# Layer 1's rows of maxima issued by another engine, and the projection of v spread over later steps

## The chip, the cores and the metric

The kernel runs on one core of one Trainium2 chip. The metric is the time of one execution on the device, in microseconds (us). Below, PE is TensorE (PEld its weight loads), DVE is VectorE, ACT is ScalarE, POOL is GpSimd and SP is SyncE. SPq and ACTq are the DMA issues of those two engines.

## What is computed

Two transformer-like layers on x of shape (8, 512, 256), in float32. This study is about layer 1's attention, which is causal and runs twice over the same keys and values:

```
qkv = xn @ Wqkv.T + b                     # 16 heads of 16 dimensions
q, k, v = split(qkv)
ctx  = causal_softmax(q @ k.T / 4) @ v
q2   = conv1d(ctx, width 3) + conv_b
ctx2 = causal_softmax(q2 @ k.T / 4) @ v
x    = x + ctx2 @ out_w.T + out_b + low_rank_ffn(xn)
```

Layer 0, which comes first, has plain attention and an eight-expert feed-forward part; the change does not touch its instructions.

## The kernel before

**Units and rounds.** Layer 1's attention is cut into 32 units: kind 1 (first attention) or kind 2 (second), batch element `b`, and half `c` (8 of the 16 heads). The order alternates two kind-1 units and two kind-2 units. `layer1` runs one round per unit and interleaves, step by step, four lanes: the exponentials of unit i (`expp`), the row maxima of unit i+1 (`maxp`), the preparation of unit i+2 (`pre1`) and the output of unit i-1 (`fin1`). A round has 22 steps. Every engine walks through the same program and issues its own part of each step, so the order of instructions on each engine's queue is the order of the steps. Within a step the lanes come in the order given.

**Preparation.** Queries and keys are float32 values split into three bf16 parts. ACT writes the high part (`high`), DVE the remainder (`residue`, L1345), POOL the two lower parts (`low`, L2014 and L2016). Then SP copies the parts into the operand tiles QA and KA by six DMAs for q and six for k (`fan`, tile t_spl to t_R; `start` at L2143 issues all DMAs of SP). A kind-1 unit also stores its split keys to memory (`ks`, one DMA behind the twelve). A kind-2 unit gets q from the convolution (L1216) and k back from `ks`. The projection of v is four parts of PE (L1197) in steps 10 to 13, and one addition of DVE (L1362) in step 14.

**Row maxima.** A unit has two halves g of 4 heads. `top` makes scores with PE (L978) and reduces them on DVE (L1387), 11 steps for each half. Then `shift` runs as a chain of its own beside the following tops: two steps later PE transposes the maxima (`turn_m`, L997) and DVE splits their negatives into three bf16 rows (`split_m`, L1401 to L1409, tile t_msp). One step after that `rows` copies the three rows into partitions 96 to 98 of QA by three DMAs of 4 KB. For half 0 this is step 14 of the round before the unit's exponentials, for half 1 step 3 of their own round. SP issues them in layer 0 and in layer 1:

```
e.wait_ge(s.msp_done, 2 * u.n + g + 1)
for x in range(3):
    self.start(m.QA[u.buf][96 + x:97 + x, 4 * g:4 * g + 4, :], m.msp[:, x, :], s.d_mq[u.buf][g])
```

**Exponentials.** PE makes the transposed scores with the rows included (`scores`, L1011, and the mask at L1015), into two banks used in turn: the scores of step k+2 wait for ACT's exponential of step k (L1812). PE's first scores of a half (steps 0 and 11) wait for that half's rows (d_mq). The sixteen products with v of a half go in one go two steps after its last scores (`product`, L1028, tile p_PV): step 12 for half 0, and step 1 of the next round for half 1. PE's `top` of step 0 waits for the copies of q and k (d_f) of the unit that follows.

Of the kernel before, what the change touches and what calls it, by code (L numbers as in the profile page):

```python
# [81 lines left out]
def packs_of(u):  # L82

    if u.causal:
        return [(0, (0, 1, 2, 3)), (1, (0, 1)), (1, (2, 3))] + [(qb, (j,)) for j in range(4) for qb in (2, 3)]
    return [(qb, (j,)) for j in range(4) for qb in range(4)]
# [76 lines left out]
def steps(n):  # L163
    for _ in range(n):
        yield
# [345 lines left out]
class Engine:  # L511
# [115 lines left out]
    def routing(self):  # L627
        return steps(46)
# [51 lines left out]
    def maxp0(self, u):  # L680
        return steps(s1_uses(u))
# [25 lines left out]
    def rows(self, u, g): pass  # L707
# [19 lines left out]
    def pre1(self, u):  # L727

        if u.kind == 1:
            yield from steps(3)  # L730
            self.part(u, 0, 0)
            yield
            self.part(u, 0, 1)
            yield
            self.high1(u, 0)
            yield
            self.rest(u, 0)
            self.part(u, 1, 0)
            yield
            self.part(u, 1, 1)  # L740
            yield
            self.fan1(u, 0)
            self.high1(u, 1)
            yield
            self.rest(u, 1)
            yield
            for k in range(4):
                self.part(u, 2, k)
                if k == 1:
                    self.fan1(u, 1)  # L750
                yield
            self.values(u)
            return
        soon = u.c or u.b not in (0, NB - 1)
        yield from steps(3 if u.c else 1 if soon else 6)
        if u.c == 0:
            for c in range(2):
                self.turn_c(u, c)
                yield
                self.keep_c(u, c)  # L760
                yield
        for i in range(6):
            self.convolve(u, i)
            if i == 3:
                self.fan1(u, 1)
            if soon or i % 2:
                yield
        self.high1(u, 0)
        yield
        self.rest(u, 0)  # L770
        yield
        self.fan1(u, 0)
        yield
# [948 lines left out]
class ScalarE(Engine):  # L1722
# [94 lines left out]
    def copy_o(self, u, g):  # L1817
# [3 lines left out]
        e.wait_ge(s.oT_mm, i - 32)  # L1821
        nc.scalar.copy(m.O[:, :], m.PV[:, :]).then_inc(s.pv_read, 1)

    def routing(self):
        e, m, s = self.e, self.m, self.s
        yield
        e.wait_ge(s.amax, 1)
        self.nc.scalar.activation(m.alpha[:, :], m.amax, ACT.Exp, scale=-1.0).then_inc(s.alpha_exp, 1)
        yield from steps(45)
# [290 lines left out]
class SyncE(Engine):  # L2120
# [59 lines left out]
    def maxp0(self, u):  # L2180
        for g in range(2):
            yield from steps(len(packs_of(u)))
            self.rows(u, g)
            yield

    def rows(self, u, g):
        e, m, s = self.e, self.m, self.s
        e.wait_ge(s.msp_done, 2 * u.n + g + 1)
        if 3 <= u.n < 16 or u.n >= 19:
            e.wait_ge(s.pv_mm, 8 * (u.n - 2))  # L2190
        for x in range(3):
            self.start(m.QA[u.buf][96 + x:97 + x, 4 * g:4 * g + 4, :], m.msp[:, x, :], s.d_mq[u.buf][g])
# [149 lines left out]
```

## Time and profile before

| | |
|---|---|
| median of 3 runs | 2215.4 us (2213.17 to 2216.7) |
| profiled execution | 2214.24 us, its span 2212.4 us |
| PE busy, share of span | 83% |
| DVE / ACT / POOL busy | 56% / 46% / 16% |
| mean granted clock of TensorE | 0.907 of full speed |
| layer 1's attention in the trace | about 1230 to 2212 us |

The span runs from the first to the last instruction; 1.8 us of the profiled execution lie around it. Shares of busy time are averages over the whole program.

### The profile page before, as it was taken

The page shows a single profiled execution, that of the slowest core. Times are in us where ns is not written, and L with a number is a line of the kernel's source. Part 1 is how long each engine was busy: PE and PEld are TensorE (multiplying, and loading weights), DVE is VectorE, ACT ScalarE, POOL GpSimd, SP SyncE. Part 2 cuts the span into 40 slices and gives each one's busy share as a digit, 9 for nine tenths or more (in the row PEclk, how much of TensorE's full clock was granted, in tenths as well). Part 3 has the DMA queues.
Part 4 walks back from the last instruction along what each step waited for, and adds up shares of the span by engine and source line. Part 5 has one row for each costly group of instructions (what it writes and reads, how often), then busy time and mean ns, then how long its engine had stood idle before and what let it go on. Part 6 is the DMA issues. An engine that isn't in the chain of part 4 may idle for free.

```text
span 2212.4 us, 31852 instructions
## 1 busy us (share of the span) xinstructions
PE 1844.8 (83%) x10767; PEld 938.3 (42%) x10777; DVE 1243.9 (56%) x3777; ACT 1016.5 (46%) x2048; POOL 364.4 (16%) x555
## 2 busy tenths in 40 slices
PE   3584899999979999993788878888878898888877
PEld 2341444554525454541233434444444444444434
DVE  4554555565554454544544656665766656565653
ACT  0232456565635555562343434444444444444434
POOL 2215211111111111114432100000100101000000
PEclk8566899999989999996898889998989998998999
DMA  7244343334374444413104424443444533543430
GB/s 144 65 151 126 73 80 69 81 73 79 61 203 64 63 64 67 63 23 93 34 19 63 61 43 66 69 64 59 63 66 67 73 55 52 74 66 52 69 44 21
DMA packets 145968, 155.87 MB, mean 70 GB/s; under 512 B 26008, under 2 KB 132784, under 8 KB 145808
## 3 DMA queue, kind: packets, MB, share of 16 engines
q1 hardware_dynamic: 123872, 114.75, 31.9%
q0 software_dynamic: 10048, 14.44, 3.6%
q10 hardware_dynamic: 11888, 24.64, 3.5%
q8 instruction: 88, 1.44, 0.3%
q14 instruction: 72, 0.59, 0.1%
HBM read 55.95 MB, written 33.72 MB: 41 GB/s over the span
## 4 chain that ended last, share of the span: by engine, by line
PE 53%; DVE 11%; SPq 11%; DMA 10%; issue 6%; POOL 6%; ACT 2%; DVEq 0%; POOLq 0%; ACTq 0%
PE p_PV L1028 11%; SPq L2143 11%; PE p_S L1011 7%; DMA t_R<-t_msp 6%; PE p_S L961 4%; PE p_Ma L1216 4%; PE p_Mb L1078 4%; PE p_S L1101 3%; DVE p_S L1387 3%; PE p_S L978 2%; POOL t_spl L2016 2%; POOL idd L2042 1%; PE p_Mb L1101 1%; DMA t_xTb<-xTd 1%; PE p_Ma L938 1%
## 5 line engine op out<-in xcount | busy, mean ns | idle before, releaser
L1812 ACT ACTIVATE t_R<-p_S 128x512 f32<-128x512 f32 (+1 forms) x1216 | 680.6, 578 | 706.3 <-PE p_S L1015 541.2
L1387 DVE CUSTOM_DVE_ANT_0 p_S<-p_S,t_NM 128x128 f32<-128x128 f32 (+3 forms) x1024 | 478.4, 514 | 347.8 <-PE p_S L978 344.3
L1011 PE MATMUL p_S<-t_R 99*128 99x512 bf16 (+3 forms) x1536 | 479.7, 337 | 100.5 <-DMA t_R<-t_msp 82.4
L1373 DVE TENSOR_REDUCE t_mx<-p_S 128x1 f32<-128x512 f32 x512 | 346.1, 685 | 257.5 <-PE p_S L961 241.1
L1028 PE MATMUL p_PV<-t_R 128*17 128x512 f32 (+3 forms) x3072 | 334.7, 561 | 1.0 <-ACT t_R L1812 1.0
L978 PE MATMUL p_S<-t_R 96*128 96x128 bf16 (+3 forms) x1024 | 264.4, 313 | 43.3 <-DVE t_mx L1387 26.0
L1011 PEld LDWEIGHTS p_S<-t_R 99*128 99x128 bf16 x1536 | 150.7, 99 | 239.1 <-DMA t_R<-t_msp 91.7
L961 PE MATMUL p_S<-t_R 96*128 96x512 bf16 x512 | 206.1, 405 | 19.9 <-DVE t_mx L1373 18.9
L2014 POOL CAST t_spl<-t_rr 128x512 bf16<-128x512 f32 x80 | 49.8, 622 | 1022.4 <-DVE t_rr L1345 1022.4
L1015 PE MATMUL p_S<-t_NM 128*128 128x128 bf16 x1024 | 203.2, 224 | 0.0
L1028 PEld LDWEIGHTS p_PV<-t_R 128*17 128x17 f32 x3072 | 77.8, 107 | 198.2 <-issue 186.7
L978 PEld LDWEIGHTS p_S<-t_R 96*128 96x128 bf16 x1024 | 88.7, 102 | 132.1 <-DVE t_mx L1387 67.6
L1387 DVE DVE_READ_ACCUMULATOR2_ANT t_mx<- 128x1 f32 x1024 | 142.4, 139 | 0.0
L961 PEld LDWEIGHTS p_S<-t_R 96*128 96x128 bf16 x512 | 50.8, 100 | 194.0 <-issue 97.5
L1015 PEld LDWEIGHTS p_S<-t_NM 128*128 128x128 bf16 x1024 | 102.5, 100 | 67.9 <-issue 44.9
L1078 PE MATMUL p_Mb<-t_R,t_NM 128*128 x184 | 97.0, 608 | 7.5 <-DMA t_NM<-hTd 3.2
L1101 PE MATMUL p_S<-t_R,t_NM 128*128 x392 | 100.9, 379 | 0.0
L1216 PE MATMUL p_Ma<-t_NM,t_R 128*128 128x512 f32 x192 | 98.1, 596 | 0.7 <-ACT t_NM L1922 0.6
L2016 POOL TENSOR_TENSOR t_spl<-t_rr,t_spl 128x512 bf16<-128x512 f32 x80 | 92.7, 1159 | 6.4
L1101 PEld LDWEIGHTS p_S<-t_R,t_NM 128*128 128x128 f32 x392 | 73.8, 190 | 17.9 <-issue 2.3
L1896 ACT ACTIVATE t_R<-p_S,t_R 128x512 f32<-128x512 f32 x64 | 43.5, 687 | 61.7 <-PE p_S L1147 51.6
L2066 POOL DMA_DIRECT2D ysd<-t_NM x39 | 34.1, 875 | 208.7 <-ACT t_NM L1868 208.7
(244 smaller groups left out, 2180.9 us busy)
## 6 DMA issues: line engine op xcount, KB each, us to landing
t_R<-t_spl SPq DMA_DIRECT2D x480, 128.0 KB
t_R<-in_w ACTq DMA_DIRECT2D x32, 512.0 KB, 7.3
t_R<-ks SPq DMA_DIRECT2D x96, 128.0 KB
ks<-t_spl SPq DMA_DIRECT2D x16, 384.0 KB, 6.9
hTd<-t_NM SPq DMA_DIRECT2D x39, 128.0 KB
ysd<-t_NM SPq DMA_DIRECT2D x39, 128.0 KB
t_NM<-hTd SPq DMA_DIRECT2D x39, 128.0 KB, 2.2
ysd<-t_NM POOLq DMA_DIRECT2D x39, 128.0 KB, 3.1
```

The costliest lines, as they stand in the source:

```text
L961: self.nc.tensor.matmul(m.S1[s1_bank(k)][:, :], qa[0:96, 4 * g + j, qb * 128:(qb + 1) * 128], ka[0:96, 4 * g + j, 0:512], start=True, stop ...
L978: t = self.nc.tensor.matmul(bank[:, z, :], qa[0:96, h, qb * 128:(qb + 1) * 128], ka[0:96, h, 0:n], start=True, stop=True)
L1011: t = self.nc.tensor.matmul(bank[:, z, :], ka[0:99, h, kb * 128:(kb + 1) * 128], qa[0:99, h, n0:512], start=True, stop=not u.causal)
L1015: t = self.nc.tensor.matmul(bank[:, z, 0:128], m.identb, m.maskk, start=False, stop=True)
L1028: t = self.nc.tensor.matmul(m.PV[32 * j:32 * j + 17, n0:512], vt[:, kb, 4 * g + j, :], m.p_tile(u, g, kb, j), start=(kb == 0), stop=(kb == 3),
L1078: z = self.nc.tensor.matmul(m.MB[i][:, :], m.hT[t % 2][:, c, :], m.W1[:, bass.ds(self.regs[t], 1), c, :], start=(c == 0), stop=(c == 1))
L1101: x = self.nc.tensor.matmul(M[:, 0:256], m.AT[:, k, :], m.W2[:, bass.ds(self.regs[t], 1), k * 256:k * 256 + 256], start=(k == 0), stop=(p ...
L1216: t = self.nc.tensor.matmul(m.MB[0][:, :], m.CW[:, i, c * 128:c * 128 + 128], m.cT[:, cc, k:k + 512], start=(i == 0), stop=(i == 5))
L1373: nc.vector.tensor_reduce(m.mx[:, g, 4 * j + qb:4 * j + qb + 1], m.S1[s1_bank(k)][:, :], AX.X, ALU.max).then_inc(s.s1_read, 1)
L1387: x = nc.vector.tensor_tensor_reduce(out=sc, in0=sc, in1=m.maskq[:, 512 - n:512], scale=1.0, scalar=NEG, op0=ALU.add, op1=ALU.max, accum_o ...
L1812: nc.scalar.activation(m.P1X[kb][ring_use(u, g, j0) % 6 if kb == 0 else j0 // per] if u.causal else m.P[p % 2][:, j0:j0 + per, :], m.s2_ba ...
L2143: self.raw.dma_start(to, of).then_inc(sem, 16)
```

## The change

`rows` in layer 1 moves from SP's queue to ACT's, with the same waits and the same three DMAs; layer 0's copy of it stays on SP under the name `rows0`. In `pre1` for kind-1 units, the four parts of the projection of v move from steps 10, 11, 12 and 13 to steps 12, 14, 16 and 18, and DVE's addition of `values` from step 14 to step 20. The copy of the keys, `fan1(u, 1)`, stays at step 11. `rest(u, 1)` stays at step 9.

```
@@ Engine.pre1, kind 1
             self.rest(u, 1)
             yield
+            yield
+            self.fan1(u, 1)
+            yield
             for k in range(4):
                 self.part(u, 2, k)
-                if k == 1:
-                    self.fan1(u, 1)
+                yield
                 yield
             self.values(u)
@@ ScalarE, new
+    def rows(self, u, g):
+        e, m, s = self.e, self.m, self.s
+        e.wait_ge(s.msp_done, 2 * u.n + g + 1)
+        if u.n >= 19:
+            e.wait_ge(s.pv_mm, 8 * (u.n - 2))
+        for x in range(3):
+            self.raw.dma_start(m.QA[u.buf][96 + x:97 + x, 4 * g:4 * g + 4, :], m.msp[:, x, :]).then_inc(
+                s.d_mq[u.buf][g], 16)
@@ SyncE
-            self.rows(u, g)
+            self.rows0(u, g)
...
-    def rows(self, u, g):
+    def rows0(self, u, g):
...
-        if 3 <= u.n < 16 or u.n >= 19:
+        if u.n >= 3:
```

## Rows read from the trace of the kernel before

**Rows 1.** The page's chain that ended last, by engine and by line.
```profile
PE 53%; DVE 11%; SPq 11%; DMA 10%; issue 6%; POOL 6%; ACT 2%; DVEq 0%; POOLq 0%; ACTq 0%
```

**Rows 2.** Waits in 1230:2212: us in total, times, longest us.
```profile
ACT t_R L1812 <- PE p_S L1015: 522.0, 397, 7.3
PE p_S L1011 <- DMA t_R<-t_msp: 82.4, 28, 5.2
```

**Rows 3.** PE's timeline at four round ends: start, duration, instruction, [idle before <-releaser].
```profile
1526.95 0.61 PE L1011 MATMUL p_S<-t_R 99*128 99x512 bf16 x1 [3.79 <-DMA t_R<-t_msp]
...
1528.56 4.26 PE L1028 MATMUL p_PV<-t_R 128*17 128x512 f32 x32
...
1587.94 0.39 PE L1011 MATMUL p_S<-t_R 99*128 99x512 bf16 x1 [1.62 <-DMA t_R<-t_msp]
...
1588.82 2.35 PE L1028 MATMUL p_PV<-t_R 128*17 128x512 f32 x32
...
1611.70 0.38 PE L978 MATMUL p_S<-t_R 96*128 96x512 bf16 x1
1616.49 0.61 PE L1011 MATMUL p_S<-t_R 99*128 99x512 bf16 x1 [4.41 <-DMA t_R<-t_msp]
```

**Rows 4.** Windows of 100, 3 and 1 us: busy, then PEclk, DMA share, GB/s.
```profile
1600.00:1700.00 100.00, 84.89 (x632) 46.42 (x634) 62.61 (x249) 44.28 (x84) 8.19 (x10) 0.91 0.49 70
...
1467.00:1470.00 3.00, 3.00 (x20) 0.99 (x24) 1.10 (x8) 1.19 (x2) 0.00 (x0) 0.60 0.00 0
...
1531.00:1532.00 1.00, 1.00 (x16) 0.28 (x12) 0.00 (x0) 0.00 (x0) 0.00 (x0) 0.50 0.00 0
```

**Rows 5.** SP's queue: start, time of the group, tile, number of DMAs.
```profile
1599.65 7.75 SPq L2143 DMA_DIRECT2D t_R<-t_spl  x12
1607.44 0.60 SPq L2143 DMA_DIRECT2D ks<-t_spl  x1
1608.09 1.81 SPq L2143 DMA_DIRECT2D t_R<-t_msp  x3
```

**Rows 6.** Windows of half a microsecond at the end of that round.
```profile
1613.50:1614.00 0.50, 0.00 (x0) 0.00 (x0) 0.00 (x0) 0.00 (x0) 0.00 (x0) 1.00 0.79 307
...
1614.50:1615.00 0.50, 0.00 (x0) 0.00 (x0) 0.00 (x0) 0.00 (x0) 0.00 (x0) 0.50 0.12 36
```

**Rows 7.** DMA to landing of three rows each, issued from 1568.1, 608.1 and 633.8.
```profile
DMA to landing us min/median/max: 1.6/1.7/1.7
...
DMA to landing us min/median/max: 4.0/4.2/4.5
...
DMA to landing us min/median/max: 7.8/7.9/8.0
```

**Rows 8.** Issues of rows on SP and of weights on ACT: ns min/median/max.
```profile
L2143 SPq DMA_DIRECT2D t_R<-t_msp x186: 502/589/1807, 1240.1 to 2181.9; - x186
...
L1774 ACTq DMA_DIRECT2D t_R<-in_w x16: 374/374/408, 148.4 to 646.2; - x16
```

**Rows 9.** Timelines of DVE and PE, steps 2 and 6 of a kind-1 round.
```profile
1593.89 0.28 DVE L1409 TENSOR_TENSOR t_msp<-t_mrr,t_msp 16x128 bf16<-16x128 f32 x1
...
1595.63 0.33 PE L1011 MATMUL p_S<-t_R 99*128 99x384 bf16 x1
```

**Rows 10.** ACT and PE, steps 4 and 5 of a kind-2 round with c = 0.
```profile
1536.43 0.49 ACT L1812 ACTIVATE t_R<-p_S 128x384 f32<-128x384 f32 x1 [0.47 <-PE p_S L1015]
1536.82 0.58 ACT L1922 COPY t_NM<-p_Ma 128x512 f32<-128x512 f32 x1
...
1537.45 1.12 PE L1216 MATMUL p_Ma<-t_NM,t_R 128*128 128x512 f32 x2
```

**Rows 11.** Steps 13 to 17, kind-1 round: DVE's last split, PE's scores of step 17.
```profile
1607.16 0.28 DVE L1409 TENSOR_TENSOR t_msp<-t_mrr,t_msp 16x128 bf16<-16x128 f32 x1
...
1607.63 0.33 PE L1011 MATMUL p_S<-t_R 99*128 99x384 bf16 x1
```

**Rows 12.** PE's groups in 1230:2212: busy us, mean ns, idle before.
```profile
L1197 PE MATMUL p_Ma<-t_WQ,t_R 128*128 128x128 f32 x224 | 34.8, 278 | 0.0
```

## Prediction

> **What bounds the kernel now.** I read the chain that ended last first. PE holds 53% of it, but SP's queue and DMA together hold 21% [rows 1]: the end is set in part by transfers and their issue. So I went to the waits in the stretch of layer 1's attention. ACT is idle for 522 us of it, always for PE's scores: that is slack, not a bound. What costs is PE's wait for the rows of maxima: 82.4 us in 28 waits, about one in each round [rows 2]. PE's timeline shows where: at step 0 of a round, before the first scores. Fourteen of the waits are long (4.41 and 3.79 us are two of them) and end the rounds that prepare a kind-1 unit; the other fourteen are short (1.62 us is one) and end the kind-2 rounds [rows 3]. By their mean the long ones make about 14 x 4.0 = 56 us and the short ones 26 us.
>
> The wait has a second price. After a long one the sixteen products take 4.26 us where they take 2.35 us after a short one [rows 3], and in that second the granted clock is 0.50, the 1.2 GHz level, where PE had been on the 2.4 GHz level before it idled [rows 4]. A stretch of 100 us with a mean clock of 0.91 has 18 us at half speed [rows 4], some 5 to 6 us a round; PE work done in it costs double. From the wait's end at 1526.95 to the end of the products at about 1532.8 [rows 3] that is 2.9 us lost.
>
> Why the rows are late: in the round that ends at 1616.49, DVE had them ready at 1607.16 + 0.28 = 1607.44 [rows 11]. SP was still issuing twelve copies of q and k, then the store of the keys, and reached the rows at 1608.09, 0.65 us late [rows 5]. That is little. The landing is what takes long: three small DMAs issued by 1609.9 let PE go on at 1616.49 [rows 3, 5], while three such DMAs on a quiet queue land in 1.7 us [rows 7]. They stand in one queue behind 1.5 MB of copies and the store.
>
> **The change: the queue.** The rows leave SP's queue for ACT's. Issue: ready by 1607.44, three issues at 589 ns each on SP [rows 8], last one out near 1609.2. An issue on ACT is shown only for weights, 374 ns [rows 8]. The rows' form is nearer to SP's figure, so I take 1.8 us for three, with 1.1 us as the lower bound. Landing beside another queue's traffic is bounded by layer 0: rows on SP with only ACT's weight loads ahead landed in 4.2 us, rows with both queues full in 7.9 us [rows 7]. I take 4 us, since ACT's queue is empty here. So the rows land at 1612 to 1613, about when PE has finished step 21 (1611.70 + 0.38) [rows 3].
>
> The Trainium skill ("DMA: Bandwidth & Descriptors", "Queues, rings and completion order") says that each DMA engine takes turns between queues, packet by packet. By that rule the landing comes out early, which the 4.2 us bear out. The same page ("Issuing engines are not separate DMA queues") says that issuing from several engines saves only issue time; by that alone the gain would be the 0.65 us a round.
>
> **What is late next.** PE's tops of step 0 need the k copies of the next unit, and these stay where they were. The data rate jumps to 307 GB/s at 1613.5 [rows 6], when only the store is left, so the copies' data ended near 1613.2. From the end of the store's data, by 1614.6 at 36 GB/s [rows 6], to PE's start at 1616.49 [rows 3] are 1.8 us, so a completion takes about that, and k arrives near 1614.8. The long wait is thus shortened by 1.7 us, not by 4.0: 14 x 1.7 = 24 us. In kind-2 rounds six copies stand directly ahead of the rows, without a store. The rows are last by little, 0.5 us as I put it: 14 x 0.5 = 7 us. Together 31 us of the 82.
>
> **The clock.** A long wait of 4 us becomes about 2, near today's short ones. A short one can lose the clock as well: in the 3 us from a start at 1467.0 it was 0.60 [rows 4], so 2.4 us at half speed and 1.2 lost by then, while the products after the short wait at 1587.94 ran in full time [rows 3]. I take 1.5 us where it falls. So 14 x (2.9 - 1.5) = 20 us come back at the long ones. At the short ones the wait sinks to near 1 us; I let ten of them keep a clock that they lose today, 10 x 1.5 = 15 us (the ten is my guess). Sum 35 us, bounds 0 and 14 x 2.9 + 15 = 56 us.
>
> **What ACT pays.** Behind the three issues on ACT stand the exponentials, and PE's scores two steps later wait for those. Half 1, step 3, kind-1 round: rows ready at 1594.17 (1593.89 + 0.28), issues until 1596.0, so the exponential of step 4 (0.49 us for this form [rows 10]) runs 1596.0 to 1596.5. PE's scores of step 6 started at 1595.63 and now wait: 0.9 us [rows 9]. ACT's high part of q and the q copies slip as much, so nothing hides it: 14 x 0.9 = 13 us. Kind-2 round with c = 0: rows ready about 1536.0, issues to 1537.9, then the exponential and the copy of L1922 of 0.58 us, which the convolution at 1537.45 needs; it starts at 1539.0 [rows 10], 1.6 us late, 8 x 1.6 = 13 us. With c = 1 the convolution's matmuls fill PE meanwhile: nothing. Half 0, step 14, kind-1: the issues end at 1609.3 and PE's scores of step 17, at 1607.63 before [rows 11], come near 1609.9. That costs nothing at the round's end while PE would otherwise wait for k there; without that cover it costs up to 1 us a round, 30 us in all. Sum 26 us; with issues of 374 ns about 12, with all 62 stalls uncovered at 1.8 us each 112.
>
> **The projection of v.** The same sixteen matmuls: 34.8 us over 14 units, 0.62 us a part [rows 12]. Three parts fewer stand ahead of step 14, so the maxima of half 0 come up to 1.3 us sooner. Parts in steps 16 and 18 fall where PE waits for the delayed exponentials. DVE's addition moves by six steps; its next reader is units away and the bank is next wanted in step 1 or 3 of the following round. I count 0, bounds -1 us and +0.5 us a round (-14 and +7). `fan1(u, 1)` stays in step 11: 0. SP loses 186 issues and its waits on the maxima; the copies wait for POOL instead, so 0.
>
> **Sum.** The profiled execution took 2214.2 us, 1.2 below the median. 2214.2 - 31 - 35 + 26 = 2174, against the median 2175.
>
> **Rivals.**
> - *The clock stays up and ACT's stall is small.* The full 56 us of clock, 31 of waits, 12 of stalls, 14 for v: 2214 - 56 - 31 + 12 - 14 = 2125; with half of these extras 2150. For it: a 2 us wait is near the ones that cost little. Against: the weights' form is not the rows'.
> - *ACT becomes the bound (slower).* Place: steps 3 and 14, where the wait for DVE and 1.8 us of issues block the exponentials. The gains are 66 us over 62 halves, so it decides from a mean loss of 1.1 us a half. With 1.5 us: 2214 - 66 + 93 = 2241. For it: only two score banks. Against: ACT idles 522 us, and the convolution and k's wait cover half of the places.
> - *The rows land no sooner.* Landing of 7.9 us from 1608.2 [rows 7] is 1616: nothing gained, 26 paid: 2240. The skill's page (first section named) says that a completion is signalled only after the earlier writes of that DMA engine in any queue; if that reached to copies still queued, this is what it would do. The row of 4.2 us was measured with two loads in flight, so it doesn't exclude it.
> - *Gain and stall cancel:* 2211 to 2219.
>
> **Numbers.** Forecast 0.45 (own range 2150 to 2200), clock and small stall 0.23, ACT bound 0.12, late landing 0.11, cancel 0.09. A difference under 0.2% can't be told from none. Faster 0.68, same 0.09, slower 0.23. The range that leaves out at most 2 in 10 goes from 2120 to 2235.
>
> **What the profile should show.** Rows' waits at step 0 mostly gone; in kind-1 rounds a wait for t_spl of about 2 us in their place; L1812 held for ACT's queue in steps 3 and 14; PE scores of L1011 waiting for L1812 by some 25 us more; products after a round's start nearer to 2.35 than 4.26 us; landing of the rows about 4 us under the copies. Wrong if the rows land in 7 us, if PE's waits for L1812 pass 60 us, or if k is there before PE.

## The result, and the profile after

| | before | after |
|---|---|---|
| median in the comparison | 2214.28 us (2211.49 to 2216.95, 8 runs) | 2202.26 us (2197.87 to 2207.88, 8 runs) |
| ratio, 95% interval | | 0.9947 [0.9934, 0.996] |
| span of the profiled execution | 2212.4 us | 2199.9 us |
| layer 1 in the trace | 1218.96 to 2212.40: 993.4 us | 1213.71 to 2199.90: 986.2 us |

The kernel is 0.5% faster, 12 us, where 40 were forecast. The direction was right and the size was not.

Two lines were added to the file ahead of these places: L1011, L1015, L978, L1028, L1216 and L1812 of before are L1013, L1017, L980, L1030, L1218 and L1814 after. L1832 is the issue of the rows on ACT's queue.

The chain that ended last, by engine, against [rows 1]:

```profile
PE 58%; DVE 12%; DMA 10%; issue 6%; ACT 4%; POOL 4%; ACTq 4%; SPq 2%; DVEq 0%; POOLq 0%
```

SP's queue fell from 11% to 2%. ACT's queue rose from 0 to 4% and ACT from 2 to 4%: part of the path moved from one issuing engine to the other. DMA kept its 10%.

Waits in 1230:2213, as in [rows 2] (us in total, times, longest us):

```profile
PE p_S L1013 <- ACT t_R L1814: 77.9, 70, 3.8
PE p_S L1013 <- DMA t_R<-t_msp: 30.9, 14, 3.5
PE p_S L980 <- DMA t_R<-t_spl: 13.5, 7, 4.4
PE p_Ma L1218 <- ACT t_NM L1933: 9.1, 7, 1.5
PE p_S L980 <- DVE t_mx L1389: 1.0, 1, 1.0
```

Before, the same five stood at 4.7, 82.4, 13.3, 0.6 and 22.9 us. The wait for the rows shrank by 51.5 us. The wait for the exponentials grew by 73.2. PE's tops waited for DVE for 22.9 us in short waits; of these one is left, since PE now stands still elsewhere meanwhile.

PE in layer 1, from its first scores to the end. First before, then after (the sixth number is the clock, behind the busy times of PE, PEld, DVE, ACT and POOL):

```profile
1218.96:2212.40 993.44, 837.92 (x6191) 447.30 (x6191) 612.70 (x2438) 444.12 (x844) 77.98 (x88) 0.92 0.40 59
```

```profile
1213.71:2199.90 986.19, 825.59 (x6191) 460.05 (x6191) 622.80 (x2438) 439.62 (x844) 77.99 (x88) 0.93 0.42 60
```

The same 6191 matmuls take 12.3 us less, and PE is idle for 160.6 us instead of 155.5. So in this pair of traces layer 1 gained 7.2 us: all of it, and more, is PE's busy time, in which the mean granted clock rose from 0.92 to 0.93, and the waits together got worse by 5. The other 5.3 us of the spans' difference arise before layer 1's first scores, where the change touches only the preparation of the first units. That start lies between 1213.5 and 1223.2 in the kernels below without any order in it, so for causes I compare layer 1's part, and for verdicts the medians. Each such part is from one execution, and the eight of the changed kernel lie 10 us apart: differences of a few us between two traces are hints and no more.

PE's timeline over the end of one round that prepares a kind-1 unit, against [rows 3]:

```profile
1505.53 0.34 PE L1013 MATMUL p_S<-t_R 99*128 99x384 bf16 x1 [0.80 <-ACT t_R L1814]
...
1519.26 0.34 PE L1013 MATMUL p_S<-t_R 99*128 99x384 bf16 x1 [1.63 <-ACT t_R L1814]
...
1524.72 0.39 PE L1013 MATMUL p_S<-t_R 99*128 99x512 bf16 x1 [2.13 <-DMA t_R<-t_msp]
...
1525.60 2.35 PE L1030 MATMUL p_PV<-t_R 128*17 128x512 f32 x32
```

The round had one long wait; now it has three shorter ones: 0.80 behind half 1's rows (an exponential that ACT ran late), 1.63 behind half 0's, 2.13 for the rows. After the last the products ran in 2.35 us, so here the clock was kept, where [rows 3] shows 4.26.

ACT and its queue in the same place:

```profile
1516.86 1.80 ACTq L1832 DMA_DIRECT2D t_R<-t_msp  x3
1518.71 1.91 ACT L1814 ACTIVATE t_R<-p_S 128x384 f32<-128x384 f32 x4 [2.41 <-issue]
```

The three issues take 1.80 us, and the four exponentials that had piled up follow at once. SP in the same round, and the landing of those rows:

```profile
1509.48 8.83 SPq L2154 DMA_DIRECT2D t_R<-t_spl  x12
1518.36 0.60 SPq L2154 DMA_DIRECT2D ks<-t_spl  x1
```

```profile
t_R<-t_msp ACTq DMA_DIRECT2D x3, 4.0 KB, 6.6
```

The last number is the median from issue to landing. The rows' own queue was empty, they were issued from 1516.86, and they landed 6.6 us later. The round of [rows 5] now reads 7.7 to 8.1 us.

Did the rows arrive sooner, then? The first copy of q is the event to count from. SP in the same round before the change:

```profile
1510.80 9.53 SPq L2143 DMA_DIRECT2D t_R<-t_spl  x12
1521.02 1.81 SPq L2143 DMA_DIRECT2D t_R<-t_msp  x3
```

The rows were issued 10.2 us after the first copy before and 7.4 us after it now, 2.8 us sooner. PE went on 16.15 us after the first copy before (1526.95, [rows 3]) and 15.24 us after it now (1524.72), only 0.9 us sooner. In the round of [rows 5] it is 16.84 against 16.82 us, and over the 14 kind-1 rounds 16.4 against 15.7 us in the mean. (A kind-1 round here is one that prepares a kind-1 unit, and a kind-2 round one that prepares a kind-2 unit.) PE's waits in these rounds fell from 4.0 to 2.2 us in the mean. So 0.7 us of that is an earlier landing. The other 1.1 us is PE coming later to the same wait, held up by its new stalls.

### The profile page after: what moved, and what is told of

The parts are those of the page before. It is cut to its first block, busy times and chain, and to the rows that moved or that the text cites. A ratio compares the mean times of both kernels' runs of the same rounds, so it can differ in the third digit from the quotient of the medians.

```text
span 2199.9 us, 31862 instructions
## 1 busy us (share of the span) xinstructions
PE 1827.9 (83%) x10777; PEld 950.1 (43%) x10777; DVE 1253.7 (57%) x3777; ACT 1011.9 (46%) x2048; POOL 364.4 (17%) x555
## 4 chain that ended last, share of the span: by engine, by line
PE 58%; DVE 12%; DMA 10%; issue 6%; ACT 4%; POOL 4%; ACTq 4%; SPq 2%; DVEq 0%; POOLq 0%
PE p_PV L1030 12%; PE p_S L1013 8%; DMA t_R<-t_msp 4%; PE p_S L963 4%; PE p_S L980 4%; PE p_Ma L1218 4%; ACTq L1832 4%; PE p_Mb L1080 4%; PE p_S L1103 3%; DVE p_S L1389 3%; SPq L2154 2%; DMA t_R<-t_spl 2%; ACT t_R L1814 2%; PE p_S L1017 1%; POOL idd L2053 1%
## 5 line engine op out<-in xcount | busy, mean ns | idle before, releaser
L1814 ACT ACTIVATE t_R<-p_S 128x512 f32<-128x512 f32 (+1 forms) x1216 | 677.4, 578 | 686.2 <-PE p_S L1017 435.8
L1389 DVE CUSTOM_DVE_ANT_0 p_S<-p_S,t_NM 128x128 f32<-128x128 f32 (+3 forms) x1024 | 483.4, 511 | 325.7 <-PE p_S L980 321.2
L1013 PE MATMUL p_S<-t_R 99*128 99x512 bf16 (+3 forms) x1536 | 493.6, 346 | 122.6 <-ACT t_R L1814 83.6
L1030 PE MATMUL p_PV<-t_R 128*17 128x512 f32 (+3 forms) x3072 | 301.1, 512 | 1.0 <-ACT t_R L1814 1.0
L980 PE MATMUL p_S<-t_R 96*128 96x128 bf16 (+3 forms) x1024 | 274.2, 321 | 21.0 <-DMA t_R<-t_spl 13.5
L1013 PEld LDWEIGHTS p_S<-t_R 99*128 99x128 bf16 x1536 | 156.0, 103 | 280.8 <-ACT t_R L1814 143.7
L1017 PE MATMUL p_S<-t_NM 128*128 128x128 bf16 x1024 | 215.2, 234 | 0.0
L1030 PEld LDWEIGHTS p_PV<-t_R 128*17 128x17 f32 x3072 | 72.2, 100 | 169.7 <-issue 156.0
L1017 PEld LDWEIGHTS p_S<-t_NM 128*128 128x128 bf16 x1024 | 108.2, 106 | 68.2 <-issue 53.4
L980 PEld LDWEIGHTS p_S<-t_R 96*128 96x128 bf16 x1024 | 90.5, 104 | 94.1 <-DVE t_mx L1389 25.0
L1218 PE MATMUL p_Ma<-t_NM,t_R 128*128 128x512 f32 x192 | 98.1, 597 | 9.1 <-ACT t_NM L1933 9.1
L1907 ACT ACTIVATE t_R<-p_S,t_R 128x512 f32<-128x512 f32 x64 | 43.5, 687 | 61.7 <-PE p_S L1149 58.4
```

Of the source, the lines that this page charges most:

```text
L980: t = self.nc.tensor.matmul(bank[:, z, :], qa[0:96, h, qb * 128:(qb + 1) * 128], ka[0:96, h, 0:n], start=True, stop=True)
L1013: t = self.nc.tensor.matmul(bank[:, z, :], ka[0:99, h, kb * 128:(kb + 1) * 128], qa[0:99, h, n0:512], start=True, stop=not u.causal)
L1017: t = self.nc.tensor.matmul(bank[:, z, 0:128], m.identb, m.maskk, start=False, stop=True)
L1030: t = self.nc.tensor.matmul(m.PV[32 * j:32 * j + 17, n0:512], vt[:, kb, 4 * g + j, :], m.p_tile(u, g, kb, j), start=(kb == 0), stop=(kb == 3),
L1218: t = self.nc.tensor.matmul(m.MB[0][:, :], m.CW[:, i, c * 128:c * 128 + 128], m.cT[:, cc, k:k + 512], start=(i == 0), stop=(i == 5))
L1389: x = nc.vector.tensor_tensor_reduce(out=sc, in0=sc, in1=m.maskq[:, 512 - n:512], scale=1.0, scalar=NEG, op0=ALU.add, op1=ALU.max, accum_o ...
```

## The experiments

**The two parts one by one.** e1 moves the rows to ACT and leaves v where it was. e2 moves v and leaves the rows on SP.

```
e1, against before:   rows on ScalarE (as in the change); pre1 unchanged
e2, against before:   pre1 as in the change; rows stay on SyncE
```

> The rows move to ACT, the projection of v stays in steps 10 to 13. Theory A (the queue does it all, v costs and gives nothing): as the changed kernel, 2202 us, -0.5% against before, PE waiting about 80 us for L1812-type exponentials. Theory B (the later parts of v are what fills PE while ACT issues): slower than the changed kernel by 5 to 15 us, 2207 to 2217, because PE's wait in step 17 grows from 1.7 us to about 2.6 us in the 14 kind-1 rounds.

> Only the projection of v moves; rows stay on SP. Theory A: no change, 2212 to 2217, the rows still land behind twelve copies and the store. Theory B: v alone carries part of the gain, 2203 to 2210, since the maxima of half 0 are ready up to 1.3 us sooner and can pass ahead of the store.

Measured: e1 2210.43 us, 0.9973 [0.9961, 0.9985]; e2 2218.5 us, 1.0018 [1.0003, 1.0032]. In e1 the wait for the rows is 25.4 us and that for the exponentials 80.1, nearly the waits of the whole change. The move of v alone gains nothing. On top of the rows' move it is worth 6 to 8 us (0.26% by the ratios, 2210 to 2202 by the medians), and the two intervals nearly touch. The time of e1 is that of theory B, but its reason is only half there: PE's stall in step 17 grows from 1.6 or 1.8 to 2.1 to 2.3 us, and the wait for the rows behind it shrinks by as much, so PE's idle time in layer 1 is the same (159.6 against 160.6 us). What differs in the two traces is PE's busy time, 833.3 against 825.6 us; why is not shown. e2 lies just above the range of its theory A. The queue is where the change acts, and where its price lies.

**Which half pays.** Half 0 on ACT, half 1 back on SP, v moved.

```
@@ e3, against after
     def rows(self, u, g):                 # ScalarE
         e, m, s = self.e, self.m, self.s
+        if g:
+            return
...
+    def rows(self, u, g):                 # SyncE
+        if g:
+            self.rows0(u, g)
```

> Half 0's rows on ACT, half 1's back on SP, v moved. Theory A (ACT's stall of half 1 is pure loss, because its rows land with eight steps to spare either way): the stalls of 0.80 us in 14 kind-1 rounds and 1.46 us in 8 kind-2 rounds go, 23 us less than the changed kernel, 2175 to 2185. Rival (what PE saves at step 3 it waits again for the copies or rows at step 0 of the next round): 2195 to 2203.

Measured: 2177.75 us, 0.9825 [0.9801, 0.9849]. PE's waits (us, times, longest):

```profile
PE p_S L1013 <- ACT t_R L1814: 60.7, 54, 4.5
PE p_S L1013 <- DMA t_R<-t_msp: 27.7, 13, 3.3
PE p_S L980 <- DMA t_R<-t_spl: 13.3, 6, 5.1
```

This is theory A's time. The wait for ACT falls by 17 us and the convolution's 9.1 us for L1933 leave the list. The rows of half 1 are not missed: they had been in time on SP. So half 1 on ACT was pure loss, 24.5 us by the medians. The forecast had priced it at 26 us (13 in step 3 and 13 at the convolution), so this is not where it fell short. Half 0 stalls PE for more: 60.7 us are left, all behind half 0's three issues or present before (4.7).

**How much the number of issues matters.** e4 sends one row instead of three (the two lower parts of the maxima are left out, and PE contracts over 97 rows instead of 99). e7 adds three more small DMAs of ACT behind each half's rows, into memory that nothing reads.

```
@@ e4, against after
-        for x in range(3):
-            self.raw.dma_start(m.QA[u.buf][96 + x:97 + x, 4 * g:4 * g + 4, :], m.msp[:, x, :])...
+        self.raw.dma_start(m.QA[u.buf][96:97, 4 * g:4 * g + 4, :], m.msp[:, 0, :])...
@@ e7, against after
+        for x in range(3):
+            self.raw.dma_start(m.scr[3 * (2 * (u.n - 16) + g) + x], m.ident[0:16, 0:64]).then_inc(s.d_scr, 16)
```

> ACT issues one row instead of three (the two lower parts of the maxima are left out, and PE contracts over 97 partitions in place of 99). It tells why rows on ACT's queue land after 6.6 to 8.1 us in kind-1 rounds. Theory A (a completion comes only when the copies issued before it, on the other queue, have landed): landing still 6 to 8 us. Theory B (the rows' packets take turns with the copies' packets, each turn costing): a third of the packets, landing 3 to 4 us. The stalls shrink from 1.8 to 0.6 us of issue: time 2150 to 2180 by both, the lower end by B.

> The changed kernel, with three further small DMAs issued by ACT behind each half's rows (256 bytes x 16 to a scratch tensor; they change nothing that is computed). It doubles ACT's blocking of about 1.8 us a half. Theory A (the blocking is paid by PE in full once it passes what the two score banks cover): 64 halves x 1.8 us = 115 us more, less what is hidden behind step-0 waits, 2270 to 2310. Rival (most of it hides): under 2250.

Measured: e4 2158.08 us, 0.9749 [0.9725, 0.9773]; e7 2284.05 us, 1.0312 [1.029, 1.0334]. The number of issues is what counts: from the change, 44 us down for two fewer a half (over 64 halves 0.69 us each) and 82 us up for three more (1.28 us each). In e7 PE waits 159 us for the exponentials, counted to the end of its longer layer 1. Both times lie in the ranges expected. (In e4 the last row is also issued 1.2 us sooner, so its 44 us need not be stall alone.) ACT is idle for half of layer 1, and still each microsecond in which its queue issues costs the kernel about 0.6 to 0.7 of one.

e4 also answers the landing. One row of 4 KB in place of three:

```profile
L1837 ACTq DMA_DIRECT2D t_R<-t_msp x1: 510/510/510, 1501.2 to 1501.2; - x1
...
DMA to landing us min/median/max: 7.0/7.0/7.0
```

A third of the data lands no sooner, as theory A has it. The time is not that of the rows' own data.

**Passing the store alone.** In the kernel before, SP issues the store of the keys (`ks`) behind half 0's rows instead of ahead of them.

```
@@ e5, against before
         for k in range(4):
             self.part(u, 2, k)
...
+            yield
+            self.keys(u)
@@ SyncE.fan
-        if u.kind == 1 and z == 1:
-            self.start(m.ks[2 * u.b + u.c], m.spl[:, 1, :, :], s.d_ks)
+    def keys(self, u):
+        self.start(m.ks[2 * u.b + u.c], m.spl[:, 1, :, :], s.d_ks)
```

> The kernel before, with one thing moved: SP issues the store of the keys in step 15, behind half 0's rows of step 14, not ahead of them. All rows stay on SP, v stays. Theory A (in kind-1 rounds the rows land when the copies ahead of them land, on either queue, so ACT's queue buys nothing there but passing the store): the kind-1 waits shrink from 4.0 to about 2 us, as in the changed kernel, and nothing is paid on ACT. 14 x 2 us of wait and 15 to 20 us of clock: 2165 to 2180. Rival (what counts is the other queue): no more than 5 us gained, 2210 to 2216.

Measured: 2201.04 us, 0.9932 [0.9918, 0.9946]. This takes one issue of 0.6 us, and 384 KB, from ahead of the rows and gives as much as the whole change, though neither expectation had this time. The wait for the rows is 70.8 us, 11.6 less, and nothing else grows. Layer 1's part is 980.9 us, 12.6 less. In the kind-1 rounds PE goes on 15.5 us after the first copy in the mean, where it was 16.4 before and is 15.7 with ACT's queue: the other queue lands the rows no sooner than SP's does without the store.

**Another queue.** All rows on POOL's queue in place of ACT's.

```
@@ e6, against after: the same three DMAs, with counters of their own
+            self.nc.gpsimd.dma_start(m.QA[u.buf][96 + x:97 + x, 4 * g:4 * g + 4, :], m.msp[:, x, :]).then_inc(
+                s.d_mr[u.buf][g], 16)
```

> All rows of layer 1 on POOL's software queue (semaphores of their own), v moved. POOL idles more than 1000 us waiting for DVE. Theory A (ACT's blocked queue is what eats the gain): PE's wait for exponentials falls from 78 to under 15 us; landing as late as on ACT in kind-1 rounds; 2160 to 2180. Rival (a software queue costs about as much somewhere else, for instance a landing later by over 2 us): 2190 to 2215.

Measured: 2187.7 us, 0.9871 [0.9855, 0.9887]. PE's waits (us in total, times, longest):

```profile
PE p_S L1020 <- DMA t_R<-t_msp: 74.4, 21, 5.9
...
PE p_S L1020 <- ACT t_R L1821: 8.9, 30, 0.4
```

The stall of ACT is gone with the queue that caused it, and PE waits for the rows instead. In a kind-1 round they were issued from 1516.3 and took 6.4 to 6.7 us: POOL's queue, empty as well, lands them no sooner than ACT's. Nor does it land them later: PE went on 15.3 us after the first copy (1508.68), as against 15.2 in the change, and its wait is longer because no stall had held it up. The time came out below the rival's range and above theory A's.

**Half 0 placed otherwise.** e8: half 1 on SP; half 0 on SP ahead of the store in rounds that prepare a kind-1 unit, on ACT in the others. e13: e3 with half 0 on ACT in the kind-1 rounds alone. e9: e3 with one row in each of steps 14, 15 and 16. e10: the changed kernel with the rows of both halves spread in that way. e11: e3 with v back in steps 10 to 13.

```
e8,  on_sync:   return g == 1 or (u.n < 47 and after[0].kind == 1)     # and the store behind the rows
e13, on_sync:   return g == 1 or u.n == 47 or after[0].kind == 2
e9, e10, shift: -        self.rows(u, g)
                -        yield
                +        for x in range(3):
                +            self.row(u, g, x)
                +            yield
e11, pre1:      as before the change
```

> Half 1 on SP; half 0 on SP ahead of the store of the keys in kind-1 rounds, on ACT only in kind-2 rounds; v moved. Theory A: the stall of 1.7 us at step 17 goes in 14 kind-1 rounds, but it was partly in the shade of the landing; 2165 to 2178, at or a little under the kernel with half 0 on ACT throughout (2177.8). Rival (SP's longer queue in kind-1 rounds delays the rows again): 2180 to 2195.

> Half 0 on ACT but one row in each of steps 14, 15 and 16, half 1 on SP, v moved. Theory A (PE pays for a block of 1.8 us because the two score banks cover only about one issue): three issues of 0.6 us hide one by one, PE's wait for exponentials falls from 61 to under 35 us, 2160 to 2172. Rival (the rows go out 1 us later and the wait at step 0 grows by what the stall loses): 2173 to 2182, as with the three in one step (2177.8).

> The changed kernel with each half's three rows spread over three steps (half 0: 14, 15, 16; half 1: 3, 4, 5), all on ACT. Theory A (the block, not ACT's total of issues, is the price): 15 to 25 us under the changed kernel, 2177 to 2190. Rival (every issue costs PE the same wherever it stands): 2198 to 2206.

> Half 0 on ACT in one step, half 1 on SP, the projection of v back in steps 10 to 13. Against the same kernel with v moved (2177.8). Theory A (v's later parts fill PE while ACT issues; alone they do nothing): 5 to 10 us slower, 2183 to 2189, as between the changed kernel and the one with only the rows moved (8 us). Rival (v's place matters only by chance of the clock): within 3 us of 2177.8.

> Half 1 on SP, half 0 on ACT in kind-1 rounds alone, on SP in kind-2 rounds; v moved. Against half 0 on ACT throughout (2177.8). It prices what the prediction set at nothing: half 0's block of ACT in kind-2 rounds. Theory A: PE's wait for exponentials falls by about 8 x 2.5 = 20 us, from 61 to near 35 to 40, its wait for rows rises by 14 x 1.7 = 24 us; the time stays within 2174 to 2186. Rival (the block in kind-2 rounds costs more than passing the copies gives): under 2172.

Measured (the last two columns are PE's waits for the rows and for the exponentials in layer 1, us):

| | median us | ratio, 95% interval | rows | exponentials |
|---|---|---|---|---|
| after | 2202.26 | 0.9947 [0.9934, 0.996] | 30.9 | 77.9 |
| e3 half 0 on ACT | 2177.75 | 0.9825 [0.9801, 0.9849] | 27.7 | 60.7 |
| e8 mixed | 2187.06 | 0.9868 [0.985, 0.9886] | 61.4 | 34.8 |
| e9 half 0, spread | 2180.13 | 0.9837 [0.9817, 0.9857] | 58.4 | 29.3 |
| e10 both halves, spread | 2188.67 | 0.9848 [0.9824, 0.9872] | 55.6 | 33.3 |
| e11 e3, v early | 2181.43 | 0.983 [0.9806, 0.9854] | 25.6 | 60.3 |
| e13 half 0 on ACT, kind-1 rounds | 2190.18 | 0.9894 [0.9875, 0.9913] | 54.0 | 33.5 |

In e3 and e9 the two waits sum to 88.4 and 87.7 us: spreading the issues turns stall into wait, one for one, in the time that e9's rival gave. In the kind-1 rounds the rows are no later for it: PE goes on 15.9 us after the first copy in the mean in both, and only comes to the wait sooner. So a stall of half 0 there costs nothing as long as the wait follows it. Where both halves are on ACT (e10) spreading pays, as its theory A has it: by the two ratios about 1% against the change. In e11 v's place makes no difference that these intervals tell (3.7 us by the medians, between its theory and its rival): once half 1 is off ACT a gain from v can't be told any more.

e8 and e13 each put half 0 back on SP in one kind of round, and both are slower than e3, by 9 and 12 us (e8's interval only just stays apart from e3's, e13's clearly). e8 fell in its rival's range, e13 above both of its ranges. So half 0 on ACT pays in either kind of round, in spite of its stalls. The sum of the two waits says little of it (96.2 and 87.5 us against 88.4). In layer 1 PE is idle for 144.3 and 143.1 us against 138.1, and busy for 825.0 and 826.4 us against 818.6. In e8 the waits for the rows in the kind-1 rounds are 3.9 to 5.4 us each, in e3 0.4 to 3.3 us. That one long stop costs more clock than two shorter ones, as in [rows 3], is how I read the busy time; no run isolates it.

**What the landing waits for.** e12 was to issue the six copies of k behind the rows by moving them from step 11 to step 15. e14 is e3 with a wait in SP's queue ahead of those copies, until half 0's maxima are split.

```
@@ e12, against after
-            self.fan1(u, 1)
...
+                if k == 1:
+                    self.fan1(u, 1)
@@ e14, against e3, SyncE.fan
+        if u.kind == 1 and z == 1 and u.n >= 18:
+            e.wait_ge(s.msp_done, 2 * (u.n - 1) + 1)
         for j, part in enumerate(of):
             self.start(to[16 * j:16 * j + 16, :, :], part, s.d_f[z][u.buf])
```

> The changed kernel with the six copies of k (and the store) issued by SP in step 15 of kind-1 rounds, not in step 11, so that only the six copies of q are ahead when ACT issues the rows of half 0. Theory A (a row is complete when the copies issued before it on the other queue are): the rows of kind-1 rounds land 2 to 4 us after issue, not 6.6 to 8.1, and PE waits for k in place of the rows. Theory B (copies issued after it hold it back as well, since they share the DMA engines): landing still 6 us or more. The time by both 2202 to 2225, since k comes later.

> Half 0 issued by ScalarE and half 1 by SyncE, as in e3; in addition SyncE's six copies of k, and the store behind them, wait until half 0's maxima are split, so that they are issued from the same moment as the rows and not up to 3 us before. In e3 such a landing took 6.6 us, with twelve copies issued before the rows. Theory (a landing grows with the copies issued before it on the other queue): the rows of kind-1 rounds have only the six copies of q ahead and land in 3 to 5 us; k is then what is late, PE's wait for t_spl takes the place of the wait for the rows (28 us in e3 become under 8, t_spl grows by 14 x 3 us or more), and the time rises to about 2200. Rival 1 (the landing is set by the bytes that move meanwhile, issued before or after): the rows still take 6.5 us or more. Rival 2 (a queue of ScalarE simply takes so long in layer 1): the same 6.6 us, to the tenth.

Measured: e12 2200.62 us, 0.9943 [0.9923, 0.9962], no different from the change. Its trace says why it tested neither theory:

```profile
1506.69 8.84 SPq L2155 DMA_DIRECT2D t_R<-t_spl  x12
1515.58 0.61 SPq L2155 DMA_DIRECT2D ks<-t_spl  x1
```

The twelve issues still run on unbroken, and stand as far ahead of the rows as in the change (issued from 1514.08, landed in 6.6 us). SP has nothing else to issue between these two steps and stops only at its waits for other engines, so here a step is an order on its queue and no time.

e14: 2169.26 us, 0.9801 [0.9783, 0.9819]. Landing of half 0's rows in the same kind-1 round, in e3 and then in e14:

```profile
L1834 ACTq DMA_DIRECT2D t_R<-t_msp x3: 510/614/616, 1513.1 to 1514.3; - x3
...
DMA to landing us min/median/max: 6.6/6.7/6.7
```

```profile
L1834 ACTq DMA_DIRECT2D t_R<-t_msp x3: 511/607/615, 1500.6 to 1501.8; - x3
DMA to landing us min/median/max: 1.6/3.4/3.9
```

Over layer 1 the kind-1 rounds between 1355 and 1880 went from medians of 6.4 to 7.8 us to 3.0 to 3.6, and the kind-2 rounds, which e14 doesn't change, kept 3.8 to 4.9 us. In e3 ten of the twelve copies had been issued when the first row was. In e14 six had been, and they had all but landed: the DMA engines moved 16 GB/s from 1500 to 1501 and 4 in the next half microsecond. The copies of k are in flight in both, but in e14 they are issued from 1500.64 on, beside the rows of 1500.60 to 1501.8 and behind them. The quickest of the three took 1.6 us, as on a quiet queue, and the others 3.4 and 3.9, while k's copies went on landing until 1509. So what a landing waits for are the copies issued before it on the other queue that haven't landed yet, and not those behind it (rival 1) nor ACT's queue as such (rival 2). PE no longer waits for rows (no such wait is left in the list); it waits for k, which now comes last:

```profile
1509.37 0.38 PE L980 MATMUL p_S<-t_R 96*128 96x128 bf16 x4 [2.77 <-issue]
```

The profile names no releaser, but the last copy of k was issued at 1504.0 and takes 5.2 us to land, which is 1509.2. There are 14 such waits, 32.8 us in all, against 27.7 for the rows in e3. My expectation of 2200 us was wrong, though the landing was right: k came 2.3 us late a round, about as late as the rows had been, not 3 us more than them. Layer 1 alone, e3 and then e14:

```profile
1220.43:2177.10 956.67, 818.59 (x6191) 458.63 (x6191) 620.69 (x2438) 441.09 (x844) 78.05 (x88) 0.93 0.42 61
```

```profile
1214.51:2166.30 951.79, 809.81 (x6191) 454.87 (x6191) 620.18 (x2438) 440.05 (x844) 77.87 (x88) 0.94 0.40 62
```

e14 is ahead by 4.9 us there, in PE's busy time, with idle time 3.9 us larger. Whether it is better than e3 their overlapping intervals don't settle; either is faster than both kernels of this study, by 1.7 to 2% against the one before and 1.2 to 1.5% against the changed one.

## Why the prediction was right in direction and wrong in size

**Bound, place and two prices: right.** The rows at step 0 were the largest wait, and half 0 alone is worth moving (e3). ACT's slack did not help it: ACT holds PE up while it issues.

**Landing, "I take 4 us": wrong.** It was 6.1 to 8.1 us in the kind-1 rounds, around the 7 us that were named there as making the prediction wrong. The bound of 7.9 us [rows 7] was the right one, and the rival "The rows land no sooner", given 0.11, had the landing right, though its 2240 us is far off, since it allowed no gain at all. The sentence that failed is "since ACT's queue is empty here": an empty queue does not help when the copies of another queue were issued first (e14: 3.4 us without k's copies ahead, 6.7 in e3 with them; e4: 7.0 us for one row). The page of the Trainium skill that the prediction set against this ("DMA: Bandwidth & Descriptors", "Queues, rings and completion order") says that a completion lands only after every earlier write of that DMA engine, across its queues; e14's 3.4 against 6.7 us agree with it. The same section's turn-taking between queues was the rule I gave the most weight; it did not bring the landing down to 4 us. No run shows the DMA engines one by one, so the mechanism inside them stays argued; the dependence on what was issued before is shown.

**Rows' wait, −31 us: too small, at −51.5.** The kind-1 waits went from 56 to 30.9 us (0.4 to 3.5 each), with the rows last and not k, so the step "k arrives near 1614.8" was never put to the test by the change. That they fell by 25 us where 24 were forecast is luck. The rows landed 0.7 us sooner a round and not 1.7, which is 14 x 0.7 = 10 us; the rest is PE coming later. The short waits in the kind-2 rounds, from which I took 0.5 us each, went altogether, 26 us: 14 waits are left of 28. Their rows had at most six copies ahead. In six of these rounds a wait of about 1 us stands in their place, five for t_spl and one for DVE. Reading one round also misled me on the issue: SP was 0.65 us late there, but 2.4 us in the round at 1521.02 (maxima ready at 1518.59). It did no harm, since the landing followed the copies and not the issue.

**ACT's stall, +26 us: right for half 1, wrong for half 0.** PE's waits for the exponentials grew by 73.2 us and the convolution's by 8.5, 82 in all; 60 was my own limit. At half 1 the priced places were right: 0.80 us for 0.9 in kind-1 rounds, 1.46 for 1.6 at the convolution, and e3 gave 24.5 us back for the 26. About 50 us more are half 0, which I set at nothing:

- Step 14 of the kind-1 rounds, "costs nothing at the round's end while PE would otherwise wait for k there". The stall is 1.6 to 1.8 us (1519.26, 1.63), where up to 1 us had been put: DVE had the maxima at 1516.83, and PE's next scores were held up by the three issues that followed. There are 14 of them, 24 us. They are given back, though by the wait for the rows and not by one for k: PE comes to it later and waits less, and DVE's maxima are ready for the tops behind it. So the cover held, as e9 shows from the other side.
- Half 0 of the kind-2 rounds, which has no term of its own and only the bound of "up to 1 us a round" over it. There PE stalls in eight waits of 2.6 to 3.8 us, 22.7 us in all, with no wait left behind them that could give it back. (Two more, of 1.8 us, come ahead of long waits for t_spl, which got shorter by 2.2 and 3.0 us.) This is the part of the term that failed: it took nearly all of the 26 us that the vanished waits of these rounds had given. PE's scores and ACT in one of them:

```profile
1581.23 0.34 PE L1013 MATMUL p_S<-t_R 99*128 99x384 bf16 x1 [2.56 <-ACT t_R L1814]
```

```profile
1578.62 2.01 ACTq L1832 DMA_DIRECT2D t_R<-t_msp  x3
1580.68 1.47 ACT L1814 ACTIVATE t_R<-p_S 128x384 f32<-128x384 f32 x3 [2.88 <-issue]
```

  ACT waited for DVE's split until 1578.59, with PE's scores of 1578.12 already there, and then issued for 2.01 us: the wait and the issues add up. That is the mechanism of the rival with ACT as the bound. The mean stall passed its measure of 1.1 us a half (82 / 62 = 1.3 us), but the kernel did not become slower, because much of the stall only took the place of other waits: 51.5 us of rows, 21.9 of DVE's waits and 12.3 of busy time went, 86 against 82.

**DVE's tops: not in the sum.** 22 us of PE's short waits for DVE vanished as longer ones took their place, which is why 82 us of new stall and 51.5 us less of waiting leave PE only 5 us more idle.

**Clock, −35 us: too large.** PE's busy time in layer 1 fell by 12.3 us. The products did gain what was promised (L1030, all of the program: us busy, mean ns):

```profile
L1030 PE MATMUL p_PV<-t_R 128*17 128x512 f32 (+3 forms) x3072 | 301.1, 512 | 1.0 <-ACT t_R L1814 1.0
```

  Before it was 334.7 us, 561 ns: 34 us less. But the same table has L1013 at 493.6 us (479.7 before), L980 at 274.2 (264.4) and L1017 at 215.2 (203.2). The stalls of 1.6 to 3.8 us stand ahead of scores, and scores were slowed in their turn (behind the one of 2.58 us at 1701.10 the first took 0.50 us, where 0.34 is usual). Clock that the change gave back at the round's end it partly lost in mid-round. (Durations in these rows overlap, so the busy time of the window is the sum to trust.)

**v, 0 us:** inside its bounds. −6 to −8 us with the rows on ACT, +4 without (e2, at the edge of the noise), nothing to be told with half 1 off ACT (e11).

**The sum redone** for layer 1: −51.5 rows, −21.9 DVE, +73.2 and +8.5 ACT, −12.3 busy time make −4.0; the rest of −7.2 are waits too small to list. Three steps of the prediction failed: the landing of 4 us, which was 6.1 to 8.1, so that the kind-1 rounds got 10 us and not 24; half 0's stall in the kind-2 rounds, set at nothing, which was 22.7 us; and the clock, 35 us of which 12 came. The rival "gain and stall cancel" (2211 to 2219) was nearer than the forecast in mechanism, though the time fell short of its range by 9 us.

## What to carry to other kernels

Ask of an engine that is to issue DMAs not how long it idles, but who needs its next instruction: here three issues of 0.6 us held up exponentials that PE needed two steps later, with the engine idle for half of the time. A small transfer is not freed by an empty queue; count the copies issued before it on any queue, and hold back those that are needed later than it. When a wait shrinks, ask whether its end came sooner or its start later: count from the event that drives it, here the first copy. A stall is free only where such a wait follows it. And move one half at a time, for one may pay while the other only costs.

## What the runs showed of the hardware

- The landing of three 4-KB DMAs on ACT's empty queue was 1.7 us with nothing before it (1622.9), 2.9 us with SP's copies just begun (1550.1), 4.6 us with five of six copies issued before it (1531.2), and 6.6 to 8.1 us with ten to twelve (1516.9 and 1605.6). One such DMA behind ten took 7.0 us (e4), and three on POOL's queue 6.4 to 6.7 us (e6).
- Issuing them holds ACT for 608 ns each in the median, near SP's 589 ns for the same form and not the 374 ns of the weights [rows 8]:

```profile
L1832 ACTq DMA_DIRECT2D t_R<-t_msp x192: 510/608/2072, 1204.0 to 2164.9; - x192
```

- In the changed kernel a wait of 2.13 us (1524.72) left the granted clock at 1.00, the 2.4 GHz level, with products in 2.35 us. Behind one of 2.08 us (1369.90) it was 0.50, the 1.2 GHz level, from 1370 to 1372, and behind one of 2.17 us (1240.49) the products took 3.11 us. In e14 one of 2.77 us was followed by products in 3.65 us (1509.96). The length of a single wait does not tell which it will be; what does, no run here shows.
